# Four banks for the first product of a routed layer: the output chunks of an item put into one PSUM bank

## The reference

```
logits  = layernorm(x) @ Wr + br            # 8 experts
e       = argmax(softmax(logits)),  p = max(softmax(logits))
h       = relu(layernorm(x) @ W1[e] + b1[e])  # 256 -> 1024
y       = h @ W2[e] + b2[e]                   # 1024 -> 256
x       = x + tanh(g_ffn[0]) * p * y
```

## Time and profile before

| what | value |
|---|---|
| median of three runs | 1979.53 us |
| span of the profiled execution | 1971.2 us |
| median of the runs less this span | 8.3 us |
| PE busy in the span | 94% |
| PEld busy | 79% |
| DVE busy | 71% |
| ACT busy | 56% |
| mean granted TensorE clock | 0.972 |

### The profile page before, as it was taken

One profiled execution on the slowest core, in us unless ns is written; L12 is line 12 of the kernel. 1 busy time (PEld: TensorE's weight loads), 2 busy tenths in 40 slices (PEclk: granted clock), 3 DMA queues, 4 the chain that ended last, 5 costly groups with the idle time before them and its releaser, 6 DMA issues.

```text
span 1971.2 us, 34855 instructions
## 1 busy us (share of the span) xinstructions
PE 1848.1 (94%) x11498; PEld 1557.3 (79%) x11498; DVE 1402.6 (71%) x2375; ACT 1094.5 (56%) x2003; POOL 730.8 (37%) x754
## 2 busy tenths in 40 slices
PE   7889996999999999999999999999998997898993
PEld 5579995877888888888888888888767997686993
DVE  4767777678777777777777777777766664866664
ACT  5548883685545555555555555455424774573771
POOL 6023331556434344353443534434002232342231
PEclk9999998999999999999999999999989999899997
DMA  4246662001000000100000000031114551203544
GB/s 126 71 144 200 200 176 76 2 17 33 17 32 16 32 32 16 32 16 32 32 16 32 21 27 32 16 116 50 30 38 150 147 147 50 71 2 118 176 138 142
DMA packets 113578, 138.95 MB, mean 70 GB/s; under 512 B 15332, under 2 KB 101606, under 8 KB 113504
## 3 DMA queue, kind: packets, MB, share of 16 engines
q1 hardware_dynamic: 105952, 121.70, 20.2%
q0 software_dynamic: 7552, 16.24, 2.8%
HBM read 117.22 MB, written 24.90 MB: 72 GB/s over the span
## 4 chain that ended last, share of the span: by engine, by line
PE 80%; DVE 10%; ACT 4%; issue 3%; DMA 2%; ACTq 0%; DVEq 0%; SPq 0%; POOL 0%; POOLq 0%
PE ps L688 43%; PE ps L949 10%; PE ps L950 10%; PE ps L951 10%; PE ps L695 2%; PE ps L882 1%; ACT ps L1595 1%; DVE xs L1799 1%; ACT wsplit L1556 1%; DVE bn L1719 1%; DVE wsplit L2180 1%; DVE lnx L1702 1%; PE ps L1149 1%; PE ps L1108 1%; DVE h_lo L2161 1%
## 5 line engine op out<-in xcount | busy, mean ns | idle before, releaser
L688 PE MATMUL ps<-h_hi,wsplit 128*128 128x512 f32 (+3 forms) x2016 | 588.5, 350 | 1.8 <-DVE xT L1947 1.3
L688 PEld LDWEIGHTS ps<-h_hi,wsplit 128*128 128x128 f32 x2016 | 366.7, 188 | 48.7 <-DVE xT L1947 1.8
L688 PE MATMUL ps<-h_lo,wsplit 128*128 128x512 f32 (+3 forms) x1008 | 352.5, 350 | 0.0
L574 POOL TENSOR_TENSOR wsplit<-wraw,zero 128x256 fp32r<-128x256 f32 (+2 forms) x160 | 150.9, 960 | 497.0 <-PE ps L951 407.7
L1477 ACT ACTIVATE lnx<-ps 128x512 f32<-128x512 f32 x384 | 229.3, 598 | 106.3 <-PE ps L951 63.6
L688 PE MATMUL ps<-xTh,wsplit 128*128 128x256 f32 (+2 forms) x992 | 254.9, 311 | 8.0 <-DVE h_lo L2161 4.4
L1486 ACT ACTIVATE h_act<-h_act 128x512 f32<-128x512 f32 x192 | 120.9, 629 | 211.8 <-DVE h_act L1925 211.7
L1947 DVE TENSOR_TENSOR xT<-xT,ps 128x1024 f32<-128x1024 f32 x124 | 151.3, 1220 | 117.7 <-PE ps L688 117.7
L1490 ACT ACTIVATE h_hi<-ps 128x512 fp32r<-128x512 f32 x256 | 152.6, 596 | 142.1 <-PE ps L688 139.8
L2161 DVE TENSOR_TENSOR h_lo<-ps,h_hi 128x256 fp32r<-128x256 f32 (+2 forms) x248 | 117.7, 475 | 151.3 <-ACT h_hi L1599 150.1
L1934 DVE TENSOR_TENSOR ps<-h_act,ps 128x512 f32<-128x512 f32 x256 | 177.4, 693 | 44.3 <-PE ps L951 30.2
(11 more groups left out here) (289 smaller groups left out, 3580.3 us busy)
## 6 DMA issues: line engine op xcount, KB each, us to landing
wraw<-in_L_w SPq DMA_DIRECT2D x124, 512.0 KB, 3.9
wraw<-in_L_ffn_Wg SPq DMA_DIRECT2D x32, 256.0 KB, 2.7
wraw<-in_L_ffn_Wu SPq DMA_DIRECT2D x32, 256.0 KB, 3.0
wraw<-in_L_ffn_Wd SPq DMA_DIRECT2D x32, 256.0 KB, 3.6
x_tok<-lnx SPq DMA_DIRECT2D x12, 512.0 KB, 4.1
lnx<-y_tok SPq DMA_DIRECT2D x12, 512.0 KB, 5.9
y_tok<-lnx SPq DMA_DIRECT2D x3, 2048.0 KB, 13.8
wat<-in_attn SPq DMA_DIRECT2D x16, 256.0 KB, 4.8
```

The costliest lines, as they stand in the source:

```text
L574: return pool.tensor_tensor(out_, in_, zero[:, :].to_broadcast(shape), ALU.add)
L688: return pe.matmul(out_, lhsT, rhs, start=start, stop=stop)
```

## The change

In layer 0 an output chunk has 256 columns, so both output chunks of an item fit into one bank of 512. They now lie side by side in bank `2 + s`. Banks 4 and 5, which this frees, go to the first product: chunk `f` has bank 0, 1, 4 or 5 in turn, and `up` waits for the chunk four before it. The first matmul that writes an item's output bank clears it; the first matmul of the second output chunk therefore comes without the start flag. Layers 2 and 3 (384 and 320 columns) keep their banks and waits.

```
+        UP_BANKS = {0: (0, 1, 4, 5), 2: (0, 1), 3: (0, 1)}
+        def up_bank(layer, f):
+            return UP_BANKS[layer][f % len(UP_BANKS[layer])]
+        def down_banks(layer, s):
+            if layer == 0:
+                return ps[:, 2 + s, :].rearrange("p (k t) -> p k t", k=KD)
+            return ps[:, 2 + 2 * s:4 + 2 * s, 0:CAP[layer]]
...
# up (TensorE)
-                    if not start or f >= 2:
-                        pe.wait_ge(f_lo, c - 1)
+                    ups = len(UP_BANKS[layer])
+                    if not start or f >= ups:
+                        pe.wait_ge(f_lo, c - ups + 1)
-                    o = ps[:, f % 2, 0:cap]
+                    o = ps[:, up_bank(layer, f), 0:cap]
...
# down (TensorE)
-                        o = ps[:, 2 + 2 * s + d, 0:cap]
-                        mm(o, whi[:, s, q, w], h_hi[:, f % 4, 0:cap], f == 0, False)
...
+                        o = down_banks(layer, s)[:, d, :]
+                        clears = f == 0 and (d == 0 or layer != 0)
+                        shared = layer == 0
+                        pe.matmul(o, whi[:, s, q, w], h_hi[:, f % 4, 0:cap], start=clears, stop=False, skip_group_check=shared)
...
# hidden (ScalarE) and lower (VectorE): ps[:, f % 2, 0:cap] becomes ps[:, up_bank(layer, f), 0:cap]
# output (VectorE)
-                    dve.tensor_tensor(y_t[:, :, 0:cap], ps[:, 2 + 2 * s:4 + 2 * s, 0:cap],
+                    dve.tensor_tensor(y_t[:, :, 0:cap], down_banks(layer, s),
```

More of the change, by code:

```diff
@@ L1136, in down @@
                         q = 2 + f // 4
-                        o = ps[:, 2 + 2 * s + d, 0:cap]
-                        mm(o, whi[:, s, q, w], h_hi[:, f % 4, 0:cap], f == 0, False)
-                        mm(o, whi[:, s, q, w], h_lo[:, f % 4, 0:cap], False, False)
-                        last = mm(o, wlo[:, s, q, w], h_hi[:, f % 4, 0:cap], False, f == FC - 1)
+                        o = down_banks(layer, s)[:, d, :]
+                        clears = f == 0 and (d == 0 or layer != 0)
+                        shared = layer == 0
+                        pe.matmul(o, whi[:, s, q, w], h_hi[:, f % 4, 0:cap], start=clears, stop=False, skip_group_check=shared)
+                        pe.matmul(o, whi[:, s, q, w], h_lo[:, f % 4, 0:cap], start=False, stop=False, skip_group_check=shared)
+                        last = pe.matmul(o, wlo[:, s, q, w], h_hi[:, f % 4, 0:cap], start=False, stop=f == FC - 1, skip_group_check=shared)
                     last.then_inc(f_used, 1)
@@ L1594, in hidden @@
                     act.wait_ge(f_up, c + 1)
-                    act.activation(ps[:, f % 2, 0:cap], ps[:, f % 2, 0:cap], func, bias=b1c[:, layer, bass.ds(ex * FC + f, 1)]).then_inc(m_act, 1)
+                    act.activation(ps[:, up_bank(layer, f), 0:cap], ps[:, up_bank(layer, f), 0:cap], func, bias=b1c[:, layer, bass.ds(ex * FC + f, 1)]).then_inc(m_act, 1)
                     act.wait_ge(m_act, MC[name] + e * FC + f + 1)
@@ L1598, in hidden @@
                         act.wait_ge(f_used, c - FH + 2)
-                    act.activation(h_hi[:, f % 4, 0:cap], ps[:, f % 2, 0:cap], ACT.Copy).then_inc(f_hi, 1)
+                    act.activation(h_hi[:, f % 4, 0:cap], ps[:, up_bank(layer, f), 0:cap], ACT.Copy).then_inc(f_hi, 1)
                 def expert(e, s, start=False, end=False):
@@ L2160, in lower @@
                     dve.wait_ge(f_hi, CHUNKS[name] + e * FC + f + 1)
-                    dve.tensor_tensor(h_lo[:, f % 4, 0:cap], ps[:, f % 2, 0:cap], h_hi[:, f % 4, 0:cap].bitcast(F32), ALU.subtract).then_inc(f_lo, 1)
+                    dve.tensor_tensor(h_lo[:, f % 4, 0:cap], ps[:, up_bank(layer, f), 0:cap], h_hi[:, f % 4, 0:cap].bitcast(F32), ALU.subtract).then_inc(f_lo, 1)
                 def output(e, s):
```

## The result

The changed kernel takes 1961.92 us (median of four runs, 1960.91 to 1963.39), against 1979.4 us (1978.5 to 1981.7) for the kernel before on the same chip: a ratio of 0.9911, 95% interval 0.9898 to 0.9923, or 17.5 us less.

A forecast was written before the change was run, and what follows sets the result against it. PE was taken to bound the kernel, losing 11.3 us in layer 0's stage to waits for DVE's `lower`. Less 0.25 us left in the first item, 1979.53 - 11.05 = 1968.5 us; own range 1965 to 1972 us, wider range 1964 to 1974 us.

The forecast's parts named there:

- The wait of `up`: Layer 0, first matmul of `up`: chain of 2.45 us against 2.13 us, short by 0.32 us; four banks remove it.
- what is late next: `down(f)` waiting for its own `lower`: 4.26 us after its `up` against a chain of 2.45 us, 1.81 us to spare.
- the first item: First item of the stage: of 2.3 us lost some 2.0 go; 0.15 us wait and 0.1 us restart stay at `down(2)`.
- The second product in one bank: `down` alternating between column halves of one bank: taken to cost nothing, bounds nothing to 19 us.
- The rival of a stall in the shared bank: Alternating column halves stall PE in each of 120 `down`s: 19 us cost at 0.16 us each, 1987.5 us; chance 0.07.
- The rule on weight loading: Steady window on PE: weight-loading share measures headroom better than matmul busy time; at most 7.5 us to win, against 2.5 us.
- After the stage, the clock: Work behind layer 0's stage moves up equally; its granted clock may change, 3 us either way.
- ACT's wait for PE: In layer 0's stage, ACT's waiting for PE shrinks from 34.2 to about 23 us.
- The sum: Whole kernel: 11.3 - 0.25 = 11.05 us gained; span 1960.2 us, time 1968.5 us with 8.3 us above the span unchanged.
- the term of 11.3 us: Layer 0's stage: 194.0 us taken against 182.7 us without waits, so 11.3 us lost.
- a gain above 14.5 us: Whole kernel: a gain larger than forecast, with only the clock as mechanism; chance 0.02.

The follow-up runs named there:

- the wait of two: Changed kernel with its four banks and shared output bank, but `up` waits for the chunk two before it: 1981.95 us, ratio 1.0012 to the kernel before.
- the shared bank alone: Changed kernel with both output chunks in one bank, but two banks for the first product as before: 1980.9 us, ratio 1.0003 to the kernel before.
- the repeat: Changed kernel once more, nothing changed in it, on the third group's chip: 1968.57 us against 1984.42 for the kernel before, ratio 0.9912.

## Why the prediction was right, and where it failed

*The wait of `up`, what is late next, the first item: right.* The wait is gone, the time did not come back at `down`, an item takes 12.23 us (12.24 predicted), and `down(2)` of the first item keeps the small remainder (the two steps of 0.16 and 0.22 us are 0.14 us over two of 0.12). The last matmul comes 182.64 us after the first `up`. With the first `up` of before (118.43) that is 301.07, where some 301.3 were predicted. That the wait alone does it, and not the banks, is shown by the pair of runs with the wait of two (1.0012) and the shared bank alone (1.0003).

*The second product in one bank: right.* Taken at nothing between 0 and 19 us; measured 1.0003 [0.9992, 1.0015], some 1 us with 2 us to either side. The rival of a stall in the shared bank is out.

*The rule on weight loading: right.* In the steady window the row of weight loading went from 166.02 to 173.41 us of 173.5 us when the waits went, while matmul busy time had only 2.5 us to gain. The window now holds 1476 matmuls in place of 1400, which at the new pace is 8.9 us of work: nearer to the 7.5 us that the row of weight loading left. The Trainium skill's page "Perfetto Trace Analysis", section "Identifying the Most-Contended Engine", prefers the former as a measure of headroom, and the trace agrees.

*After the stage, the clock: within its bounds.* The granted clock of the stretch that follows is 1.00 in place of 0.96, and 0.79 in place of 0.78 at its start. Behind the stage no time was won or lost: from the last `output` to the end of the span there are 1658.4 us before and 1658.5 us after. The span gained 10.2 us where the stage gained 11.3 us because the stage began 1.0 us later (118.58 against 117.59), not because of what follows it.

*ACT's wait for PE: off.* 17.6 us against some 23 us. With ACT's loops written out, where one stop of 0.9 us is left, it is 22.7 us: ACT's own stops stand in part where it would have waited for PE. No time hangs on it.

*The sum: this step failed.* "The median of the runs lies 8.3 us above the span; with these unchanged the time is 1979.53 - 11.05 = 1968.5 us." Around a span lie 1.8 us. The other 6.5 us were no fixed part: the profiled execution was that much shorter than the timed ones (1971.2 + 1.8 = 1973.0 us, below each of the 25 runs of the kernel before on the chip of the first group of experiments, 1977.9 us the lowest). So the term of 11.3 us, the loss that the change removes, was read from an execution that had less of it. The other three traces in which `up` waits for the chunk two before it, with nothing else changed on ACT or DVE, have a stage of 200.4 to 201.1 us, where the first has 195.2 us. Against the 183.9 us of four banks that is a loss of 16.5 to 17.2 us, and the runs say 17.5 us (15.9 us in the repeat). With 5.2 to 5.9 us more, the same sum gives 1962.6 to 1963.3 us; 1961.92 us was measured. What the prediction lacked was the late start of ACT's `rows_upper`, which two banks pass on to PE in part: with the loops written out these stops shrink, and the stage of two banks loses 4.0 of the 5.9 us. The prediction gave a gain above 14.5 us a chance of 0.02 "and no mechanism but the clock".

Two things in this stay inferred. That the timed executions of before had the longer stage is taken from the traces of other executions, since none at the median was traced. And spans can't settle it: what follows the stage takes 1657 to 1669 us in the traces of all these runs, with two banks as with four, a spread as large as the gain in question.

That four banks also hide the late instructions is shown in the changed kernel's own trace. Timeline around a stop of ACT of 1.38 us: `rows_upper` is late, `rows_lower` and the `lower` behind it start at 160.00 and 160.76, and PE goes on with a `down` at 160.59 without a wait. (`rows_lower` is listed with `issue`, but starts 0.03 us after `rows_upper` has ended: it waited for ACT.)

```profile
157.60 0.39 ACT L1611 ACTIVATE h_hi<-ps 128x256 fp32r<-128x256 f32 x1
...
159.37 0.60 ACT L1602 ACTIVATE xTh<-ps 128x512 fp32r<-128x512 f32 x1 [1.38 <-remote]
...
160.00 0.69 DVE L2169 TENSOR_TENSOR xTl<-ps,xTh 128x512 fp32r<-128x512 f32 x1 [0.42 <-issue]
...
160.59 0.28 PE L1150 MATMUL ps<-h_hi,wsplit 128*128 128x256 f32 x1
...
160.76 0.42 DVE L2173 TENSOR_TENSOR h_lo<-ps,h_hi 128x256 fp32r<-128x256 f32 x1
```

## What to carry to other kernels

A buffer that an engine waits for is worth the mean shortfall of the chain behind it, and also every irregular delay in that chain: here 11.3 us of regular wait and over 5 us from late instructions went with the same two extra banks. So count the spare time a deeper rotation leaves, not only the wait it removes. When the median of the runs lies further above the profiled span than an execution spends around its span, the profiled execution was a short one. The surplus sits in some stage, perhaps in the one that is changed, as here, perhaps in another, as in the run with four banks and the wait of two; only a second trace of the stage tells. Until then it belongs in the range, on the side of the gain.

## What the runs showed of the hardware

Two accumulations that alternate between the column halves of one bank run at the same 0.12 us a matmul of 256 columns as those in banks of their own.

An engine's instruction can come late with nothing that the profile shows holding it: 0.85 to 1.6 us, once in each pass of a loop, on ACT ahead of `rows_upper`. The profile may list such a stop as a wait for an instruction that ended more than 1 us earlier. With ACT's loop written out, four stops of up to 1.1 us are left; with the loops of all three engines written out, six of at most 0.3 us, and the two-bank stage is 4.0 us shorter. With 1.05 us of added work at that place the stops are not listed, and the time stays as it was (0.9993). One execution of the kernel before had none of them. What makes the instructions late was not tried beyond this.
